# An S4D long convolution and a quantised feed-forward block: gate and up weights turned by DMA transposes instead of TensorE and ScalarE, and the down weights' scales made one iteration earlier

## The reference, cut to what matters

```python
def cond(u, ..., length):                       # u = x
    K  = get_kernel(...)                        # [64 heads, 1024]
    y  = irfft(rfft(u, n=2 * L) * rfft(K, n=2 * L))[..., :L] + u * D[:, None]
    return y * (arange(L) < length[:, None])[:, None, :]

def fake_quant(t, axis):                        # value: q
    s = maximum(max(abs(t), axis, keepdims=True) / 127.0, 1e-8)
    return clip(round(t / s), -128, 127) * s

def qlinear(x, w):                              # w is [out, in]
    return einsum('bsh,oh->bso', fake_quant(x, -1), fake_quant(w, 1))

def ffn(x, w_gate, w_up, w_down):               # [2752, 1024], [2752, 1024], [1024, 2752]
    h = silu(qlinear(x, w_gate)) * qlinear(x, w_up)
    return qlinear(h, w_down)

out = x + ffn(cond(x, ...), w_gate, w_up, w_down)
```

## Time and profile before

| | us |
|---|---|
| median of 3 runs | 1289.55 |
| lowest, highest | 1288.41, 1290.99 |
| the profiled execution: its own time | 1293.98 |
| the profiled execution: span | 1292.2 |
| TensorE busy | 1236.7 (96%) |
| VectorE busy | 921.0 (71%) |
| ScalarE busy | 406.2 (31%) |
| GpSimd busy | 331.7 (26%) |
| mean DMA rate | 126 GB/s |

### The profile page before, as it was taken

One profiled execution on the slowest core, in us unless ns is written; L12 is line 12 of the kernel. 1 busy time (PEld: TensorE's weight loads), 2 busy tenths in 40 slices (PEclk: granted clock), 3 DMA queues, 4 the chain that ended last, 5 costly groups with the idle time before them and its releaser, 6 DMA issues.

```text
span 1292.2 us, 19618 instructions
## 1 busy us (share of the span) xinstructions
PE 1236.7 (96%) x6559; PEld 671.3 (52%) x6654; DVE 921.0 (71%) x1543; ACT 406.2 (31%) x588; POOL 331.7 (26%) x318
## 2 busy tenths in 40 slices
PE   2899999999899999999999999999999999999998
PEld 0676777766664444444444444444444444444443
DVE  7799998978768665566666566667656667655666
ACT  3344544445542222232222222222222222222321
POOL 1233434323431112122111222211222211121220
PEclk9999999999999999999999999999999999999999
DMA  3599999988863232323332233233222333323224
GB/s 103 177 271 269 284 274 287 286 266 279 284 211 80 52 84 63 71 67 73 79 80 70 63 71 71 69 79 87 63 67 67 75 72 84 76 63 71 68 65 104
DMA packets 141001, 162.26 MB, mean 126 GB/s; under 512 B 104796, under 2 KB 105006, under 8 KB 139694
## 3 DMA queue, kind: packets, MB, share of 16 engines
q1 hardware_dynamic: 140974, 161.92, 46.3%
HBM read 113.31 MB, written 25.49 MB: 107 GB/s over the span
## 4 chain that ended last, share of the span: by engine, by line
PE 80%; DVE 8%; issue 5%; DMA 4%; ACT 1%; SPq 1%; POOL 1%; DVEq 0%; ACTq 0%; POOLq 0%
PE bank L1069 45%; PE bank L1083 21%; PE bank L850 10%; DMA chunk<-in_x 2%; PE bank L867 1%; PE bank L836 1%; DVE tail L796 1%; DVE tail L774 1%; PE bank L1086 1%; DMA rows<-in_x 1%; DVE w_max L741 1%; POOL w_int L634 0%; ACT wd L687 0%; DVE w_max L746 0%; PE bank L1096 0%
## 5 line engine op out<-in xcount | busy, mean ns | idle before, releaser
L1069 PE MATMUL bank<-wgu,rows 128*128 128x512 bf16 (+1 forms) x3009 | 596.9, 356 | 3.3
L1069 PEld LDWEIGHTS bank<-wgu,rows 128*128 128x128 bf16 x3072 | 291.2, 98 | 308.5 <-issue 6.8
L1126 DVE SCALAR_TENSOR_TENSOR chunk<-bank,sx_all,wide 128x512 f32<-128x512 f32 (+1 forms) x288 | 198.5, 708 | 251.1 <-PE bank L1069 251.1
L1230 POOL TENSOR_TENSOR w_int<-chunk,rounder 128x512 bf16<-128x512 f32 x186 | 174.4, 952 | 688.7 <-ACT chunk L1206 686.0
L1200 ACT ACTIVATE chunk<-chunk 128x512 f32<-128x512 f32 x192 | 112.4, 585 | 589.6 <-DVE chunk L1126 589.6
L1083 PE MATMUL bank<-wd,tail 128*128 128x512 bf16 x1271 | 284.3, 379 | 1.6
L850 PE MATMUL bank<-chunk 128*128 128x512 f32 (+7 forms) x1024 | 263.1, 410 | 0.1
L850 PEld LDWEIGHTS bank<-chunk 128*128 128x128 f32 x1024 | 176.2, 191 | 85.0 <-issue 54.4
L1083 PEld LDWEIGHTS bank<-wd,tail 128*128 128x128 bf16 x1302 | 127.0, 98 | 146.3
L634 POOL TENSOR_TENSOR w_int<-wide,rounder 128x1024 bf16<-128x1024 f32 (+1 forms) x68 | 130.0, 1921 | 230.3 <-ACT wide L666 158.2
L1206 ACT ACTIVATE chunk<-chunk,h_inv 128x512 f32<-128x512 f32 x192 | 118.5, 665 | 80.5 <-DVE h_inv L1147 80.5
(11 more groups left out here) (137 smaller groups left out, 598.8 us busy)
## 6 DMA issues: line engine op xcount, KB each, us to landing
chunk<-k_rev SPq DMA_DIRECT2D x64, 512.0 KB, 6.2
tail<-in_x SPq DMA_DIRECT2D x62, 256.0 KB, 3.9
out_x<-tail SPq DMA_DIRECT2D x62, 256.0 KB, 3.2
wide<-in_L_ffn_w_gate SPq DMA_DIRECT2D x22, 512.0 KB, 6.7
wide<-in_L_ffn_w_up SPq DMA_DIRECT2D x22, 512.0 KB, 8.9
wide<-in_L_ffn_w_down SPq DMA_DIRECT2D x8, 1376.0 KB, 7.4
chunk<-in_x SPq DMA_DIRECT2D x34, 256.0 KB, 6.6
rows<-in_x SPq DMA_DIRECT2D x32, 256.0 KB, 6.2
```

Source lines behind the costliest of these rows:

```text
L1069: last = pe.matmul(bank[:, 0:n], xq[:, par, c, :], wgu[:, NC - 1 - c, first + cols.start:first + cols.stop], start=(c == 0), stop=(c == NC ...
L1126: dve.scalar_tensor_tensor(out=buf[j % 2][:, 0:n], in0=bank[:, 0:n], scalar=sx, in1=s[:, cols], op0=ALU.mult, op1=ALU.mult).then_inc(gu_sc ...
L1230: pool.tensor_tensor(h_int[:, piece(j)], h[:, par, piece(j)], rounder[:].to_broadcast([P, n]), ALU.subtract).then_inc(h_int_ready, 1)
```

## The change

The gate and up pieces are turned by `dma_start_transpose`, issued by SP from `w_int` straight to `wgu` (`move_w`). TensorE's `turn_w` and ScalarE's `place_w` remain for the down weights alone and count their own pieces (`down_pieces`). GpSimd waits for `w_moved[k]` before it writes a half of `w_int` again. In SP's list the first transpose stands ahead of the gate load, the second ahead of the up load, and the down load moves ahead of the first Toeplitz load. `scale_w` of the down weights moves from the middle of iteration i - 1 to the end of iteration i - 2. The diagonal matrix goes away: TensorE turns the broadcast inverse by one transpose. SP's wait for the stored scales moves to the load that reads them, SP waits for all transposes before iteration 23, and SP's loop over the iterations is unrolled.

```diff
+    def down_pieces(i, k):
+        return BATCHES * (i - DOWN_FIRST) + k if isinstance(i, int) else BATCHES * i + k - BATCHES * DOWN_FIRST
...
     # run(): loops of all engines but SP
-        with eng.Fori(DOWN_FIRST, WEIGHT_ITERS - 3, 2) as i:
-            body(i, DOWN_FIRST % 2)
-            body(i + 1, 1 - DOWN_FIRST % 2)
-        for i in range(WEIGHT_ITERS - 2, TILES):
+        body(DOWN_FIRST, DOWN_FIRST % 2)
+        with eng.Fori(DOWN_FIRST + 1, WEIGHT_ITERS - 4, 2) as i:
+            body(i, 1 - DOWN_FIRST % 2)
+            body(i + 1, DOWN_FIRST % 2)
+        for i in range(WEIGHT_ITERS - 3, TILES):
             body(i, i % 2)
...
     # SP
+        def move_w(i, k):
+            sp.wait_ge(w_int_ready, pieces(i, k) + 1)
+            first = row_of(i) + k * F
+            sp.dma_start_transpose(wgu[:, :, first:first + P], w_int[:, k * L:(k + 1) * L]).then_inc(w_moved[k], 16)
+
         def body(i, par):
 
             if gate_stage(i):
+                move_w(i, 0)
                 if has(i, GU_ITERS - 2):
-                    sp.wait_ge(w_int_ready, pieces(i, 0) + 1)
                     load_gu(i + 2, par, 0)
             if has(i, TILES - 2):
 
                 sp.wait_ge(x_turned, 2 * i + 2)
                 load_x(i + 2, par)
-
-                sp.wait_ge(conv_done, 2 * i + 1)
-                load_t(i + 2, par, 0)
             if down_stage(i) and has(i, WEIGHT_ITERS - 2):
                 sp.wait_ge(w_int_ready, pieces(i, BATCHES))
                 load_down(i + 2, par)
-            if gate_stage(i) and has(i, GU_ITERS - 2):
-                sp.wait_ge(w_int_ready, pieces(i, 1) + 1)
-                load_gu(i + 2, par, 1)
+            if has(i, TILES - 2):
+
+                sp.wait_ge(conv_done, 2 * i + 1)
+                load_t(i + 2, par, 0)
+            if gate_stage(i):
+                move_w(i, 1)
+                if has(i, GU_ITERS - 2):
+                    load_gu(i + 2, par, 1)
...
+                sp.wait_ge(s_stored, 64)            # now ahead of the load of the scales
...
-                sp.wait_ge(s_stored, 64)            # was in store_scales(0)
...
-        run(sp, body, lambda: store_scales(0))
+        for i in range(DOWN_FIRST):
+            body(i, i % 2)
+        store_scales(0)
+        for k in range(2):
+            sp.wait_ge(w_moved[k], 16 * GU_ITERS)
+        for i in range(DOWN_FIRST, TILES):
+            body(i, i % 2)
...
     # GpSimd, unround()
-            if turned is not None:
-                pool.wait_ge(w_turned, turned)
+            if gate_stage(i):
+                if not isinstance(i, int) or i >= 1:
+                    pool.wait_ge(w_moved[k], 16 * i)
+            else:
+                if k < 2 and isinstance(i, int) and i == DOWN_FIRST:
+                    pool.wait_ge(w_moved[k], 16 * GU_ITERS)
+                if not isinstance(i, int) or i > DOWN_FIRST:
+                    pool.wait_ge(w_turned, down_pieces(i - 1, k) + 1)
...
     # ScalarE, place_w(): gate and up branch out
-            if gate_stage(i):
-                dst = wgu[:, :, bass.ds(row_of(i) + k * F, P)]
-                act.activation(dst, ps_w[k][:], ACT.Copy).then_inc(w_placed, 1)
-                return
...
     # VectorE
-            dve.tensor_scalar(diag[:], ident[:], t_inv[:], None, ALU.mult).then_inc(diag_ready, 1)
...
-            elif not gate_stage(i) and has(i, WEIGHT_ITERS - 1):
-                scale_w(i + 1, 1 - par)
             mask_y(i, par, 1)
...
             if gate_stage(i) and has(i, GU_ITERS - 2):
                 first_max(i + 2, par)
+            elif not isinstance(i, int) or DOWN_FIRST - 2 <= i < WEIGHT_ITERS - 2:
+                scale_w(i + 2, par)
...
     # TensorE
         def spread_inv(i):
-            pe.wait_ge(diag_ready, i + 1)
-            pe.matmul(ps_i[:], ones[:], diag[:], start=True, stop=True).then_inc(inv_spread, 1)
+            pe.wait_ge(scale_step, 4 * i + 3)
+            pe.transpose(ps_i[:], t_inv[:].to_broadcast([P, P]), ident[:]).then_inc(inv_spread, 1)
...
-                if gate_stage(i) or down_stage(i):
-                    turn_w(i, par, hh if gate_stage(i) else 2 * hh)
-                    if hh == 0 and not gate_stage(i):
+                if not gate_stage(i) and down_stage(i):
+                    turn_w(i, par, 2 * hh)
+                    if hh == 0:
                         turn_w(i, par, 1)
```

More of the change, by code:

```diff
@@ L430, in convolve_and_pack @@
     xq = tail[:, 2 * L:2 * L + L // 2].bitcast(BF16).rearrange("p (c t) -> p c t", c=NC)
-    y_max, diag = tail[:, 5 * L // 2:5 * L // 2 + P], tail[:, 5 * L // 2 + P:5 * L // 2 + 2 * P]
+    y_max = tail[:, 5 * L // 2:5 * L // 2 + P]
     t_max = sb("t_max", [P, 1])
@@ L449, in convolve_and_pack @@
     scale_step = sem("scale_step")
-    diag_ready = sem("diag_ready")
     inv_spread = sem("inv_spread")
@@ L460, in convolve_and_pack @@
     w_int_ready = sem("w_int_ready")
+    w_moved = [sem(f"w_moved{k}") for k in range(2)]
     w_turned = sem("w_turned")
@@ L618, in on_gpsimd, with unround @@
     def on_gpsimd(pool):
-        def unround(i, par, k, turned):
+        def unround(i, par, k):
             if gate_stage(i):
@@ L635, in unround @@
                                ALU.subtract).then_inc(w_int_ready, 1)
-        unround(0, 0, 0, None)
+        unround(0, 0, 0)
         def body(i, par):
             if gate_stage(i):
[L641 to L649, removed]
+                unround(i, par, 1)
+                if has(i, GU_ITERS - 1):
+                    unround(i + 1, 1 - par, 0)
+            else:
+                if down_stage(i):
+                    unround(i, par, 2)
+                if has(i, WEIGHT_ITERS - 1):
+                    unround(i + 1, 1 - par, 0)
+                    unround(i + 1, 1 - par, 1)
         run(pool, body)
@@ L675, in place_w @@
         def place_w(i, par, k):
-            if isinstance(i, int) and i == 0 and k == 0:
-                act.wait_ge(k_stored, 80)
-            act.wait_ge(w_turned, pieces(i, k) + 1)
-            if gate_stage(i):
-                dst = wgu[:, :, bass.ds(row_of(i) + k * F, P)]
-                act.activation(dst, ps_w[k][:], ACT.Copy).then_inc(w_placed, 1)
-                return
+            act.wait_ge(w_turned, down_pieces(i, k) + 1)
             bank = ps_w[(BATCHES * down_slot(par) + k) % 2]
@@ L695, in body @@
         def body(i, par):
[L696 to L701, removed]
             if has(i, TILES - 1):
@@ L712, in body @@
                 round_down(i + 1, 1 - par)
-            if gate_stage(i):
-                place_w(i, par, 0)
             if gate_stage(i):
@@ L854, in turn_w @@
         def turn_w(i, par, k):
-            m = pieces(i, k)
-            pe.wait_ge(w_int_ready, m + 1)
+            m = down_pieces(i, k)
+            pe.wait_ge(w_int_ready, pieces(i, k) + 1)
             if not isinstance(i, int) or m >= 2:
                 pe.wait_ge(w_placed, m - 1)
[L861 to L865, removed]
+            cols = turn_cols(k)
+            bank, start, stop = ps_w[(BATCHES * down_slot(par) + k) % 2], cols.start, cols.stop
             for c, f in enumerate(range(start, stop, P)):
@@ L874, in spread_inv @@
         def spread_inv(i):
-            pe.wait_ge(diag_ready, i + 1)
-            pe.matmul(ps_i[:], ones[:], diag[:], start=True, stop=True).then_inc(inv_spread, 1)
+            pe.wait_ge(scale_step, 4 * i + 3)
+            pe.transpose(ps_i[:], t_inv[:].to_broadcast([P, P]), ident[:]).then_inc(inv_spread, 1)
         def turn_scales(first, n, at, steps):
-            pe.wait_ge(diag_ready, at)
+            pe.wait_ge(scale_step, 4 * at)
             pe.wait_ge(w_step, steps)
@@ L921, in convolve_and_pack @@
                 w_int=w_int, conv_done=conv_done, y_masked=y_masked, w_placed=w_placed, rows_loaded=rows_loaded, scales_loaded=scales_loaded,
-                w_pieces=GU_UNITS + BATCHES * DOWN_TILES)
+                w_pieces=BATCHES * DOWN_TILES)
 def tile_slots(rows, chunks):
```

## The result

| | us |
|---|---|
| before, median of 6 runs | 1290.7 |
| after, median of 6 runs | 1282.46 (1280.47 to 1283.68) |
| ratio | 0.9937, 95% interval 0.9926 to 0.9948 |
| profiled execution after: own time, span | 1283.68, 1281.7 |
| predicted | 1332 (1304 to 1364) |

First the page of the changed kernel: busy time, and the DMA and rate rows of its 40 slices, for the earlier trace rows.

The account below looks back on a forecast made before the run. Gate/up was taken as bound almost equally by TensorE (10.05 us) and DMA (9.8 us), the down stage by a ring. 1293.98 + 52 (gate/up) - 9.4 (down) = 1336.6 us, median 1332, range 1304 to 1364.

Parts of the forecast that it names:

- Step 3: Gate/up stage: DMA work of 12.4 us per iteration at share 0.98 makes the pitch 12.7 us, +52 us.
- The bounds: Gate/up pitch: 11.6 us (+28) if a tenth of the present DMA work gives way, 14 (+81) if transposes stretch.
- rival A: Gate/up DMA share is occupancy, not a limit; transposes slip in, VectorE sets 9.5 us, median 1262; chance 0.11.
- Rival B: Gate/up Toeplitz and x packets get quicker beside transposes: pitch 11.0 to 11.8 us, median 1295 to 1312; chance 0.14.
- step 1: Gate/up stage: transposes leave TensorE and the spread becomes one transpose, taking TensorE from 10.05 to 9.0 us per iteration.
- step 2: Gate/up stage: 16 transposed blocks add 2.6 us of DMA time per iteration, at about 200 GB/s.
- Step 4: SP's gate/up list: 8-block transpose issues take 1.3 us, at worst 2.4; total at most 6.6 or 8.8, under 12.7.
- Step 5: GpSimd waits for transposes to land before overwriting w_int: ring of 11.2 to 12.2 us, under the pitch, costed at nothing.
- Step 6: Down stage: earlier maximum and scale of weights cut the ring, pitch 11.92 to 10.75 us, -9.4 us (0 to -12).
- Step 7: Peeled and unrolled loops, the moved wait for stored scales and the earlier first two down scales cost nothing.

Follow-up runs that it names:

- experiment 6: Kernel before, TensorE still turning all weights, with plain copies of each w_int half to wd added where the changed kernel has transposes; 1338.67 us, ratio 1.0383.
- experiment 11: Changed kernel with the load of x moved ahead of the first transpose and the gate load; 1279.61 us, ratio 0.9914 to before.
- Experiment 1: Kernel before with only the down weights' part of the change, TensorE still turning gate and up weights; 1283.62 us, ratio 0.9943.
- experiment 12: Changed kernel with only gate weights turned by DMA, up weights by TensorE and ScalarE, and x loaded before transpose and gate load; 1267.61 us, ratio 0.9829.

## Why the prediction was wrong

**Step 3 failed**, "DMA work per iteration becomes 9.8 + 2.6 = 12.4 us". The second term was right: a transposed packet of 256 bytes took 18.5 ns, 2.4 us for 16 blocks. The first was taken as nearly a constant and is not one: between 82 and 233 us plain work fell from 9.9 us per iteration to 8.4 (125.8 us of packet time over 15 iterations). And all of it, 10.8 us, runs at a share of 1.08 in this stretch, not 0.98, so in 10.0 us. For copies the sum came out (12.3 us, experiment 6), for transposes it did not. The bounds allowed a tenth of elasticity; it was 15%, and the share gave another 9%, which is the kind of rival A. Rival B had the right kind with too small a size (11.0 to 11.8 us) and named the pitch, 10.75, at which it would cancel the down gain; with 10.3 that gain was left whole. The range, from 1304 us on, held less than half of rival B's 1295 to 1312, not most of it.

**Steps 1 and 2** held: 9.2 us for TensorE against 9.0, and 256 bytes in 18.5 ns on each of 16 engines, 221 GB/s, against the 200 that step 2 went by. The page "Advanced Engine Details and Errata" of the Trainium skill, section "X-Bar Transpose (TRN2)", says that a transposing DMA is as fast as a regular one. The trace does not agree: plain packets of 4096 bytes in 193 ns are 340 GB/s.

**Step 4** was too low: an 8-block issue took 1.92 us in the median and up to 3.40, not 1.3, and SP's issues fill 7.7 us of each 10.1. SP still rests 2 us an iteration, but the load of x behind the transpose had its price: ahead of it the kernel is 2.9 us faster (experiment 11).

```profile
L553 SPq DMA_TRANSPOSE wgu<-w_int x44: 1253/1916/3398, 52.9 to 271.8; - x44
```

**Step 5**: GpSimd does wait for the landing, 60.2 us in 16 waits between 82 and 233 us, and in that stretch no TensorE instruction waits for GpSimd. GpSimd's 1.9 us and the median landing of 7.3 us make a ring of 9.2 us and more, so it has little slack at 10.0 us.

**Step 6** was right: -10.05 us over seven pitches, where 7 x 1.17 = -8.2 was forecast. Experiment 1 shows that it stands alone, with -7.65 of the 10.05. **Step 7** had nothing for iteration 22, which became 1.58 us longer at a granted clock of 0.84. In the gate/up stage TensorE's own sum fell by 0.9 us an iteration, as step 1 said, and none of it came through.

## What the runs showed of the hardware

Shown: in this kernel 8-block and 4-block DMA transposes in a full queue make the plain loads beside them quicker, the more so the more blocks are turned, up to 16 an iteration (232 to 192 ns); plain SBUF copies hardly do (223 ns). The blocks are not all of it: with 8 an iteration the packet time was 211, 205, 202 and 189 ns in four kernels. Only argued: that transposes do it by holding the engines together. For it speaks this stretch of the changed kernel. At 67.2 us one DMA engine is taken by a 16 KB instruction fetch for 1.1 us; at the next transpose 21 of its packets take 1.1 to 1.3 us each where 18.5 ns is the mean (share 2.49), and then hardly anything is moved.

```profile
70.00:71.00 1.00, 0.55 (x5) 0.41 (x4) 1.00 (x2) 0.00 (x0) 0.00 (x0) 1.00 0.97 332
71.00:72.00 1.00, 0.00 (x0) 0.00 (x0) 1.00 (x2) 0.00 (x0) 0.00 (x0) 1.00 2.49 217
72.00:73.00 1.00, 0.82 (x8) 0.82 (x8) 1.00 (x2) 0.05 (x1) 0.00 (x0) 1.00 0.13 25
```

The same follows the fetches at 240.7 and 270.3 us, in the pitches of 12.07 and 12.42 us. With copies (experiment 6) no packet of over 1 us follows within 5 us of a fetch. Against too simple a picture: in experiment 12 transposed packets of up to 1.6 us stand at 170 us, with no fetch of 16 KB in the 100 us before. Why loads in step should be quicker, and why twice the transposes lose the effect, stays open.

## What to carry to other kernels

A busy share near 1 says that a queue is full, not that its work is a fixed sum, nor that 1 is its limit: before adding up packet times, look whether the same load has a quicker rate elsewhere in the trace (here 410 GB/s against 278). In this queue 2.6 us of DMA transposes an iteration cost 0.2 us and 3.0 us of copies 2.2 us, so the kind of an added transfer matters more than its own time. SP's issue time of a DMA transpose grew from 1.24 us on a quiet queue to 1.9 and 2.9 us in full ones; it belongs in the sum. Where two engines stand at almost the same height, split the work between them and bring the load that both wait for to the front; here one gave 5.5 us, the other 2.9, and both 14.9.
